# Attention kernel, opening: a second key chunk and four extra-row copies held, one value piece moved

## The reference

```python
q = heads(hidden_states @ W_q)
k_t = heads(text_ehs @ W_k)
v_t = heads(text_ehs @ W_v)
scores_t = einsum('bhsd,bhtd->bhst', q, k_t) * attn_scale
probs_t = softmax(scores_t, axis=-1)
text_out = einsum('bhst,bhtd->bhsd', probs_t, v_t)
attn_scores = einsum('bhsd,bhnd->bhsn', q, heads(ip_ehs @ W_k_ip)) * attn_scale
qsem = l2norm(einsum('bhst,bte->bhse', probs_t, text_ehs))
sem = einsum('bhse,bne->bhsn', qsem, l2norm(ip_ehs))
probs_ip = softmax(attn_scores + 0.5 * sem) * spatial_mask[None, None, :, None]
out = text_out + einsum('bhsn,bhnd->bhsd', probs_ip, heads(ip_ehs @ W_v_ip))
out = out @ W_out + b_out + residual
```

## Time and profile before

| | us |
|---|---|
| median of 3 runs | 729.2 |
| lowest, highest | 726.13, 729.36 |
| the profiled execution | 730.1 |
| its span, first to last instruction | 728.3 |
| PE busy | 714.9 |
| DVE busy | 633.2 |
| ACT busy | 560.7 |
| POOL busy | 441.3 |

### The profile page before, as it was taken

How to read it: one execution, slowest core, us unless ns; L and a number is a source line. 1 busy time by engine, 2 the same in 40 slices (tenths; PEclk the granted TensorE clock), 3 DMA queues, 4 the chain that set the end, 5 groups by cost and what they waited for, 6 DMA issues and landing times.

```text
span 728.3 us, 22685 instructions
## 1 busy us (share of the span) xinstructions
PE 714.9 (98%) x7260; PEld 566.1 (78%) x7260; DVE 633.2 (87%) x1879; ACT 560.7 (77%) x1611; POOL 441.3 (61%) x563
## 2 busy tenths in 40 slices
PE   8899999999999999999999999999999999999997
PEld 6677778787887878878787887878788787788764
DVE  5478898989889898998989899898988989899986
ACT  5377787787878878787887878788787877878783
POOL 6435657566565656656566665656666565666684
PEclk9899999999999999999999999999999999999999
DMA  7775664352625435272542636345262543417001
GB/s 246 149 172 121 144 110 114 54 112 72 139 75 88 115 50 116 75 143 68 91 120 42 124 73 122 89 66 122 58 130 77 107 98 59 106 25 139 15 1 21
DMA packets 135355, 70.13 MB, mean 96 GB/s; under 512 B 75352, under 2 KB 134792, under 8 KB 135240
## 3 DMA queue, kind: packets, MB, share of 16 engines
q1 hardware_dynamic: 130856, 65.60, 42.2%
q10 hardware_dynamic: 4064, 2.73, 1.4%
q0 software_dynamic: 320, 0.36, 0.3%
HBM read 41.94 MB, written 15.24 MB: 79 GB/s over the span
## 4 chain that ended last, share of the span: by engine, by line
PE 91%; DMA 3%; DVE 2%; POOL 2%; issue 1%; ACT 0%; SPq 0%; POOLq 0%; ACTq 0%; DVEq 0%
PE ps_gram L888 18%; PE ps_prep L771 18%; PE ps_pT L871 12%; PE ps_gram L889 12%; PE ps_score L858 6%; PE ps_prep L832 5%; PE ps_val L897 4%; PE ps_val L898 2%; PE ps_prep L829 1%; PE ps_prep L802 1%; PE ps_prep L804 1%; DMA w_raw<-in_L_xattn_W_k_ip 1%; PE ps_prep L944 1%; DMA q_st<-q_bounce 1%; POOL dual L624 1%
## 5 line engine op out<-in xcount | busy, mean ns | idle before, releaser
L624 POOL TENSOR_TENSOR dual<-prob 128x371 f32<-128x371 f32 (+1 forms) x288 | 251.3, 873 | 257.9 <-ACT prob L1165 257.7
L888 PE MATMUL ps_gram<-gram_hi,pT_hi 125*128 125x371 f16 (+1 forms) x864 | 273.1, 321 | 2.1 <-DVE pT_lo L1385 1.7
L889 PE MATMUL ps_gram<-gram_lo,pT_hi 125*128 125x371 f16 (+2 forms) x864 | 230.6, 267 | 0.0
L1159 ACT ACTIVATE pT_hi<-ps_pT 125x384 f16<-125x384 f32 (+1 forms) x279 | 134.7, 483 | 108.4 <-PE ps_pT L871 99.1
L1149 ACT ACTIVATE prob<-ps_score,low 128x371 f32<-128x371 f32 (+1 forms) x288 | 165.4, 574 | 26.9 <-DVE low L1380 21.6
L1385 DVE TENSOR_TENSOR pT_lo<-ps_pT,pT_hi 125x384 f16<-125x384 f32 (+1 forms) x279 | 150.2, 538 | 29.7 <-ACT pT_hi L1159 25.4
L1380 DVE TENSOR_REDUCE low<-ps_score 128x1 f32<-128x371 f32 (+1 forms) x288 | 154.7, 538 | 18.5 <-PE ps_score L858 14.2
L1398 DVE CUSTOM_DVE_ANT_0 quad_junk<-ps_gram,dual 128x371 f32<-128x371 f32 (+1 forms) x288 | 152.9, 531 | 6.0 <-POOL dual L624 1.9
L897 PE MATMUL ps_val<-val,pT_hi 125*128 125x84 f16 (+3 forms) x864 | 152.3, 196 | 0.0
L1165 ACT ACTIVATE prob<-prob 128x371 f16<-128x371 f32 (+1 forms) x288 | 151.2, 525 | 0.1
L898 PE MATMUL ps_val<-val,pT_lo 125*128 125x42 f16 (+3 forms) x864 | 141.1, 181 | 0.0
(11 more groups left out here) (280 smaller groups left out, 1520.4 us busy)
## 6 DMA issues: line engine op xcount, KB each, us to landing
ctx_sb<-in_ctx_t SPq DMA_DIRECT2D x15, 750.0 KB, 4.8
w_raw<-k_bounce SPq DMA_DIRECT2D x32, 216.0 KB, 4.0
k_st<-k_bounce SPq DMA_DIRECT2D x28, 216.0 KB, 4.0
k_bounce<-k_hi SPq DMA_DIRECT2D x15, 288.0 KB, 4.2
k_bounce<-k_lo SPq DMA_DIRECT2D x15, 288.0 KB, 4.3
q_st<-q_bounce SPq DMA_DIRECT2D x60, 63.0 KB, 2.4
xt_sb<-in_x_t SPq DMA_DIRECT2D x16, 168.0 KB, 5.5
w_raw<-k_hi SPq DMA_DIRECT2D x32, 84.0 KB, 3.0
```

Source lines behind the costliest of these rows:

```text
L624: nc.gpsimd.tensor_tensor(dual[0:r, t % 2, :], prob[0:r, g % 4, 0:TX], prob_16[0:r, t % 2, :], ALU.subtract).then_inc(s_dual, 1)
L888: nc.tensor.matmul(ps_gram[t % 2][:, 0:TX], hi, gh[0:TROWS[i], i, :], start=(i == 0), stop=False, skip_group_check=True)
L889: last = nc.tensor.matmul(ps_gram[t % 2][:, i * TC:TX], hi, gl[0:TROWS[i], i, i * TC:TX], start=False, stop=(i == NT - 1), skip_group_chec ...
```

## The change

SP waits for all twelve DMAs of `s_first` before it sends the second key chunk out. POOL waits for the same before it issues its four extra-row key copies. On PE the third value piece (`PIECES_V[2]`) is no longer made ahead of the first score but between score 1 and the turning of probabilities 0; there it takes the place of the eight warm-up transposes. ACT and DVE evict it there too: ACT after its first two exponentials, DVE after its first two minima. The warm-up transposes ahead of score 0 go from 28 to 6.

```diff
-WARM_UP, STAY_WARM, WAIT_WARM, EXP_WARM = 9, 16, 28, 8
+WARM_UP, STAY_WARM, WAIT_WARM = 9, 16, 6
@@ SP
             bring_k(start, s_first, 0, XP, stores=1)
+            sp.wait_ge(s_first, 2 * FIRST - 16 * 4)
             bounce_k(start, PIECES_K[1], 1, CC)
@@ POOL
                     stack_q_extra(pool, start, term, 0, s_pool_q[term])
+            pool.wait_ge(s_first, 2 * FIRST - 16 * 4)
             for term in (0, 2, 1, 3):
                 stack_k_extra(pool, start, term, 1, s_pool_k[term])
@@ PE
-            for k in PIECES_V:
+            for k in PIECES_V[:2]:
                 make(start, k, SETUP_BANKS)
...
             scores(start, 0)
             scores(start, 1)
-            stay_warm(EXP_WARM)
+            make(start, PIECES_V[2], SETUP_BANKS)
             transposes(start, 0)
@@ ACT
-            for k in PIECES_V:
+            for k in PIECES_V[:2]:
                 make_hi(start, k, SETUP_BANKS)
...
             exps(start, 1)
+            make_hi(start, PIECES_V[2], SETUP_BANKS)
             split_hi(Batch(1, 1, 0), PIECE_X)
@@ DVE
-            for k in PIECES_V:
+            for k in PIECES_V[:2]:
                 make_lo(start, k, SETUP_BANKS)
             minimum(start, 0)
             minimum(start, 1)
+            make_lo(start, PIECES_V[2], SETUP_BANKS)
             for k in DVE_PIECES:
                 split_lo(Batch(1, 1, 0), k)
```

## The result

The changed kernel takes 729.8 us (median of 15 runs, 727.88 to 731.82); the kernel before, run beside it on the same chip, takes 726.2 us (median of 15, 724.72 to 729.36). The ratio is 1.0044, interval 1.0032 to 1.0055: 3.6 us lost, where 2.3 were forecast as won. The profiled execution of after is 729.93 us (span 728.0, mean granted clock 0.994), at its own median. The profiled execution of before, on which the whole prediction was built, is 730.1 us, 3.9 above the median that its kernel turns out to have. In a later set of 25 runs of before, 20 had a mean clock of 0.999 or more (median 726.0) and five a lower one (728.3 to 730.8). Over the three later sets, 81 runs, eight took 729.2 us or more, three of these at a mean clock of 1.000: the page described one of a rare kind, and a low clock is not the only way to it.

The account below looks back on a forecast made before the run. PE, 91% of the last chain, was taken as the bound, its first score waiting for a crowded Q stacking. Landing -3.9, value piece +2.1 and clock -0.5 gave -2.3 us, 729.2 to 726.9; range 723.9 to 730.5.

Parts of the forecast that it names:

- The sum: Whole kernel: landing -3.9, value piece +2.1, clock afterwards -0.5, together -2.3 us from 729.2, giving 726.9; chance 0.50.
- the landing: Opening: with both holds the last Q stacking lands at 28.0 instead of 31.9; 3.9 us gained.
- the value piece: After the first score: the moved piece makes pT_lo 2.1 us later if the clock falls, 0.9 at full clock.
- the clock afterwards: After pT_lo: PE works 1.6 us instead of 3.6 at half speed, worth 1.0 or 0; 0.5 us gain taken.
- (c): SP's queue: batch 2's text too late if issued after 37.2; 729.1 us, 730.5 with the landing at 29.3; chance 0.11.
- (b): Opening: the landing moves only half way, to 29.3, as a slow engine may set its end; 728.3 us; chance 0.15.
- Behind POOL's wait: Opening: POOL's four issues (to 30.1), two text splits (to 31.8), x split and first dual stay hidden; no cost.
- The small Q copies are issued while the copy out is under way, as before: SP's queue after its wait: issuing these copies adds no delay; stackings go at 32.6, batch 2's text at 36.8.
- (d): Opening: first stacks still land at 31.9, piece wholly at half clock, pT_lo 2.1 to 2.6 later; 731.5 us; chance 0.05.
- (a): Opening: the clock stays at 2.4 GHz, so the value piece costs 0.9; -4.8 in all, 724.4 us; chance 0.19.

Follow-up runs that it names:

- before's second: The kernel before, unchanged, profiled once more: 725.61 us (median of 10), ratio 1.0004; the profiled execution took 725.75 us.
- the last kernel: The kernel before with POOL's hold alone, POOL's splits behind DVE's, batch 2's text loaded ahead of the bias, 14 warm-ups: 724.78 us, ratio to before 0.9969.
- e12: The changed kernel, with POOL waiting behind its four issues for DVE's splits of batch 1's text: 728.07 us, ratio to before 1.0026.
- e1: The changed kernel, with DVE's two splits of batch 1's text behind tile 0's pT_lo and the third minimum: 727.21 us, ratio to before 1.0007.
- e5: The kernel before with the two holds alone, 6 warm-ups, and POOL's splits waiting for DVE's splits of batch 1's text: 728.67 us, ratio to before 1.0024.
- e2: The kernel before with the two holds alone, third value piece ahead of the first score, 6 warm-ups instead of 28: 729.41 us, ratio to before 1.0048.
- e4: The changed kernel, with POOL's two text splits of batch 1 ahead of its wait and four key copies: 728.22 us, ratio to before 1.0019.

## Why the prediction was wrong, point by point

**The sum.** It was -3.9 for the landing, +2.1 for the value piece and -0.5 for the clock afterwards. Against a typical execution of before, the same terms are -1.9, +1.05 and +2.3, and one that the sum had at nothing is +2.5: DVE's splits held by POOL. Together +3.9. That 729.8 lies within the stated range is luck: the case at that end of the range, (c), names a wait for batch 2's text that cost nothing in after.

**The baseline.** "The profiled execution is 730.1 us (span 728.3), 0.9 above the median 729.2 of the three runs." The three runs were few; with 15 the median is 726.2. The page showed an execution with a first score 2.4 us late and a fall of the clock, together 4.4 us. The forecast's gain was computed against that state. Even so measured it isn't there: against the profiled before, after's fifth score is 0.4 us earlier, not 2.3. Against the typical one it is 3.9 later.

**The landing**: expected at 28.0, measured 27.60, and the last Q stacking took 2.78 us (2.5 in the uncrowded case of the earlier trace rows). The mechanism holds: it was a crowd, and rival (b) falls; what it drew from the turns that the DMA engines take, that emptying the other queues would give only part of the time, these runs don't bear out. The term of the sum was mis-sized all the same, 3.9 on paper and 1.9 against a typical opening. Counted from POOL's first Q copy it is 2.4 to 4.2 (10.12 or 11.90 to 7.74). The estimate from the Trainium skill (DMA: Bandwidth & Descriptors, Anatomy of one DMA), 2.15 us, was short by 0.6; that fit is for transfers that GpSimd issues, and this one went out on ACT's queue.

**"Behind POOL's wait ... PE and DVE are not there before 33: hidden."** This is the step that failed. It asked who waits for POOL's results, not what POOL's instructions do to a neighbour while they run. And DVE was there before 33 by the prediction's own numbers: with pT_lo ending 5.8 us after 28.0, its splits stand at about 32.2 to 33.2 (31.0 to 32.1 at full clock), while POOL, free of issues at 30.1, has 1.7 us of text splits, the x split (0.8) and the dual (0.9) to do, until 33.5. POOL's text splits, which in both profiles of before were over by the time DVE began its own, were put on top of them: 2.5 us, on the path of pT_lo. The evidence: splits of 3.04 and 3.95 us end 0.42 us behind POOL's last instruction (after, the holds alone); 1.00 once POOL stands behind DVE, with the change otherwise whole (4.5 us to pT_lo, the 4.6 of the prediction's sum at full clock); 1.62 with POOL's hold gone.

**The value piece**: 0.9 at full clock was right (1.05 measured with the rest of the path); the sum took 2.1, for a fall of the clock during the piece that did not come. But it also moves DVE's splits against POOL's x split and dual, 0.6 us, which the sum lacked: of the 2.5 us, 0.6 stay when POOL's hold is gone (1.62 for the two splits), and 1.9 are the hold's.

**The clock.** "The idle time is as long as before, so I take the fall." It did not fall there: after went through 2.28 us at full level and fell in the 4.38 us that the held splits made. Over all profiles: the four with idle times of PE of 1.03 us and less around the first scores (before's second, POOL behind DVE with the holds alone and with the queue mended, the last kernel) stay at 1.00; each of the others idles 1.9 to 4.4 us once or twice and has a stretch at 1.2 GHz, at the first score (2.30 with DVE's splits last, 2.28 with POOL's first, 2.18 with the transposes), or not there but later (2.28 and 2.98 with no fall, then 4.38 with one; 2.35 with none, then 1.89 with one). So the same idle time was followed by either level; what decides stays open. The low stretch behind pT_lo costs 2.3 us against an execution that has none, where the sum gave 0.5 back.

**(c), the text on SP's queue.** The mechanism is real and the point was set too kindly: issued at 38.66 in after, beyond the 37.2, it cost nothing there, because everything was late (landed 44.4, taken at 46.18). As soon as the splits are out of POOL's way it takes 2.05, 2.27 and 4.15 us of ACT (e12, e1, e5).

```profile
28.56 2.80 SPq L338 DMA_DIRECT2D q_st<-q_hi  x2
31.40 2.24 SPq L338 DMA_DIRECT2D q_st<-q_lo  x2
33.68 2.53 SPq L344 DMA_DIRECT2D k_st<-k_bounce  x4
...
38.66 0.38 SPq L377 DMA_DIRECT2D ctx_sb<-in_ctx_t  x1
```

In after (above) the four small Q copies took SP 5.0 us to issue; in the typical before 2.7. "The small Q copies are issued while the copy out is under way, as before" failed by 2.3 us, and the text went out 1.9 us later than the 36.8 of the sum. **(d)** is excluded by 27.60. **(a)**, the clock staying up, is what most executions of before do already, so it was not a gain to be had.

## To carry over

Before a wait is put on an engine, list its later instructions by time, and ask of each not only who waits for its result but which instruction of DVE it will lie beside. Compare the profiled execution with the median of many runs and read its granted clock before its waits are taken for the kernel's. And a hold pays where it clears the crowd and delays nothing: here POOL's, with its own computing sent behind DVE's. SP's hold bought about 0.7 us of landing (8.44 to 7.74) and made its in-order queue keep back what the next batch wants (4.15 us of ACT's waiting in e5); that it costs more than it buys is likely by these numbers, but no pair of runs shows it in the time.

## What the runs showed of the hardware

**DVE and POOL on SBUF.** A DVE instruction of 0.54 us was held for 3.04 and 3.95 us by POOL's back-to-back run, whose four instructions take 0.82 to 0.88 each. Both its inputs are in SBUF. With one input in PSUM nothing is held: all 288 pT_lo of the changed kernel take 0.49 to 0.56 us, many of them beside POOL's computing. And a single POOL instruction holds a small one with two SBUF inputs until it ends (78.16 and 78.14):

```profile
77.25 0.89 POOL L626 TENSOR_TENSOR dual<-prob 112x371 f32<-112x371 f32 x1 [0.40 <-ACT prob L1167]
77.43 0.73 DVE L1411 TENSOR_TENSOR nrm<-meta,rsum 112x14 f32<-112x14 f32 x1
```

The Trainium skill (SBUF — State Buffer, SBUF: two separate sides) has this: the port pair that DVE shares with GpSimd is an exclusive lock; of a DVE instruction with two SBUF inputs and a GpSimd instruction that reads SBUF, the one that starts first gets the pair for the whole instruction, and the other blocks. By that rule one POOL instruction should cost the split under 0.9 us. The trace agrees on the lock and goes further: DVE did not get its turn between two of POOL's, and in e2 its split is recorded as starting 0.22 us ahead of POOL's first (29.24, 29.46) and was held all the same. Where only the x split and the dual were near, DVE did get its turn between the two (in e4 its splits end at 35.57, 0.42 behind the x split's end at 35.15, while the dual runs to 36.31), and both sides lengthened, DVE's splits by 0.6 us together, POOL's x split by 0.4. Why it did there and not in the long run stays open.

**POOL's DMA issues don't hold DVE**: one split of 0.54 us (e2) and two of 1.00 us together (e5) beside them, with the transfers in flight.

**POOL's four extra-row copies made most of the crowd**: 8.3 to 8.4 us from POOL's first Q copy to the first score with them held alone (336 KB), 9.1 with SP's two 192 KB copies held alone, 10.1 to 11.9 with neither.
